# A graph attention layer: more of each tile's neighbour slots weighted by ScalarE, fewer by VectorE

## The reference

```
h = relu(layernorm(x))
g = (h @ W.T) as 8 heads of 32
score[i,j,head] = g[i].a_src + g[j].a_dst + adj[i,j]*We + be, only where adj[i,j] > 0
p = softmax over j of leaky_relu(score, 0.2)
out = x + sum_j p[i,j,head] * g[j,head,:] + h @ Wr.T + br
```

## Time and profile before

| | before |
|---|---|
| median of 3 runs | 2985.23 us (2981.51 to 2986.05) |
| profiled execution: its time | 2983.55 us |
| profiled execution: its span | 2982.0 us |
| mean granted TensorE clock | 0.682 of full speed |
| DVE busy over the span | 2407.1 us, 81% |
| POOL busy | 2003.5 us, 67% |
| ACT busy | 1625.0 us, 54% |
| PE busy | 1586.4 us, 53% |

### The profile page before, as it was taken

The page is one execution under the profiler, slowest core; times in us unless marked ns, Lnnn a source line. Parts: engine busy times, 40 slices in busy tenths (PEclk is TensorE's granted clock), DMA queues, the critical chain, the costliest instruction groups (busy, mean ns, idle before and its releaser), DMA issues.

```text
span 2982.0 us, 31982 instructions
## 1 busy us (share of the span) xinstructions
PE 1586.4 (53%) x5859; PEld 1067.1 (36%) x5860; DVE 2407.1 (81%) x5721; ACT 1625.0 (54%) x6849; POOL 2003.5 (67%) x1931
## 2 busy tenths in 40 slices
PE   7970043333436444565556666565656564526666
PEld 4650043323324332343333333333333332315445
DVE  3549576667868777899999999999999999189992
ACT  2220022223347555677778887786878775725444
POOL 3664777777777777777777777777777765254540
PEclk9995576666756666666666666666665666658888
DMA  3454533445454655566666767666666664264550
GB/s 98 147 184 139 174 110 109 115 121 161 130 158 140 182 161 170 163 196 198 194 197 196 217 205 214 203 206 209 208 208 212 206 205 145 106 166 106 130 141 2
DMA packets 254494, 486.91 MB, mean 163 GB/s; under 512 B 119232, under 2 KB 150464, under 8 KB 252144
## 3 DMA queue, kind: packets, MB, share of 16 engines
q1 hardware_dynamic: 151280, 319.60, 35.2%
q0 software_dynamic: 84752, 148.94, 18.8%
q10 hardware_dynamic: 18288, 16.65, 1.8%
HBM read 549.09 MB, written 25.76 MB: 193 GB/s over the span
## 4 chain that ended last, share of the span: by engine, by line
issue 29%; DMA 26%; POOL 20%; DVE 13%; PE 7%; ACT 2%; POOLq 1%; SPq 0%; DVEq 0%; ACTq 0%; PEldq 0%
DMA gath<-table,offs 24%; POOL gath L413 20%; DVE work L526 2%; PE banks L946 2%; DVE work L522 2%; DVE uleak L716 2%; DVE ushift L714 2%; PE banks L940 2%; ACT gath L808 2%; DMA adj_sb<-in_adj_dram 1%; PE banks L943 1%; DVE gath L698 1%; PE banks L1027 1%; PE banks L1017 1%; DVE adj_sb L698 1%
## 5 line engine op out<-in xcount | busy, mean ns | idle before, releaser
L413 POOL DMA_INDIRECT gath<-table,offs x1637 | 1718.6, 1050 | 604.8 <-issue 408.2
L808 ACT ACTIVATE gath<-gath,prob 128x32 f32<-128x32 f32 x6416 | 1366.4, 307 | 110.3 <-DVE prob L625 110.3
L969 PE MATMUL banks<-gath,ident 128*128 128x256 f32 x1670 | 513.3, 480 | 892.7 <-DVE gath L637 892.7
L976 PE MATMUL banks<-gath,ident 128*128 128x256 f32 x1604 | 630.0, 513 | 281.4 <-ACT gath L808 281.1
L969 PEld LDWEIGHTS banks<-gath,ident 128*128 128x128 f32 x1670 | 408.9, 249 | 1014.4 <-DVE gath L637 935.8
L526 DVE FIND_INDEX8 work<-work,adj_sb 128x8 uint32<-128x176 f32 (+30 forms) x833 | 645.5, 797 | 0.7 <-issue 0.6
L522 DVE MAX8 work<-adj_sb 128x8 f32<-128x176 f32 (+30 forms) x833 | 593.3, 788 | 11.0 <-DMA adj_sb<-in_adj_dram 11.0
L976 PEld LDWEIGHTS banks<-gath,ident 128*128 128x128 f32 x1604 | 327.9, 234 | 555.9 <-ACT gath L808 536.9
L803 ACT ACTIVATE prob<-pre 128x176 f32<-128x176 f32 (+23 forms) x63 | 23.7, 376 | 850.9 <-DVE pre L615 850.1
L437 POOL TENSOR_TENSOR gath<-gath 128x4096 f32<-128x4096 f32 x16 | 152.1, 9528 | 189.5 <-DMA gath<-dst_rows 189.5
L637 DVE TENSOR_TENSOR gath<-gath,prob 128x1024 f32<-128x1024 f32 (+8 forms) x171 | 240.2, 1456 | 2.1 <-issue 0.2
(11 more groups left out here) (111 smaller groups left out, 1788.5 us busy)
## 6 DMA issues: line engine op xcount, KB each, us to landing
adj_sb<-in_adj_dram SPq DMA_DIRECT2D x504, 512.0 KB
gath<-dst_rows SPq DMA_DIRECT2D x16, 2048.0 KB, 8.8
gath<-table,offs POOLq DMA_INDIRECT x1637
table<-gath POOLq DMA_DIRECT2D x32, 264.0 KB, 2.9
gath<-in_x_dram SPq DMA_DIRECT2D x32, 256.0 KB, 3.0
resid<-gath POOLq DMA_DIRECT2D x32, 256.0 KB, 2.6
work<-table SPq DMA_DIRECT2D x8, 1024.0 KB, 8.8
res_sb<-resid ACTq DMA_DIRECT2D x63, 128.0 KB
```

What stands on the lines that cost most here:

```text
L413: pool.indirect_dma_start(gath[:, ph.slot(b, k), :], None, table[:, :], bass.IndirectOffsetOnAxis(ap=offs[:, b, k:k + 1], axis=0), bounds_ ...
L808: last = s.activation(g, g, ACT.Copy, scale=prob[:, k * H + h:k * H + h + 1])
L969: last = m.matmul(ps_sum[:, b, :], ident[:, :], gath[:, ph.slot(b, k), 0:HD], start=False, stop=False)
L976: last = m.matmul(ps_sum[:, b, :], ident[:, :], gath[:, ph.slot(b, k), 0:HD], start=False, stop=(k == K - 1))
```

## The change

`act_slots` follows one formula instead of four cases, and the exponential gets one more wait.

```diff
-        self.act_slots = 10 if self.K < 20 or self.K > 38 else 14 if self.K < 32 else 16
+        self.act_slots = min(self.K // 2 + 6, 18)
```

```diff
                 c, K = j + ph.c0, ph.K
+                if ph.act_before:
+                    act.wait_ge(S["act_weighted"], ph.act_before)
                 act.wait_ge(S["z_ready"], c + 1)
                 s.activation(prob[:, 0:K * H], pre[:, b, 0:K * H], ACT.Exp).then_inc(S["exped"], 1)
```

## The result

The changed kernel took 3016.82 us (median of 4 runs, 3014.53 to 3020.07), against 2985.1 us of the kernel before in the same session: a ratio of 1.0116, with a 95% interval of 1.0104 to 1.0128. The kernel is 31.7 us slower; the prediction said 45.6 us slower, and its range of 3014 to 3046 holds the time.

The account below looks back on a forecast made before the run. The prediction took GpSimd to bound tiles 1 to 18 and, after the change, ScalarE from tile 19 on. Its terms -5.4 + 6.5 + 24 + 20.5 + 0 summed to +45.6 us, a median of 3031 us, range 3014 to 3046.

Parts of the forecast that it names:

- What bounds what: GpSimd's gathers set the pace in tiles 1 to 18, VectorE from tile 29 on; tiles 19 to 28 lie between.
- the handover: ScalarE's time between two tiles' weightings: copy, store, exponential and VectorE's normalization; 2.2 us for K of 20 to 23, 2.1 below.
- +24: Tiles 29 to 60: ScalarE becomes later than VectorE, making the stretch 24 us longer, bounds +20 and +30.
- ScalarE's cycle: Tiles 29 to 60: ScalarE's time per tile, slots of 1.704 us plus 2.2 us, 31.2 us with 17 slots.
- Tiles 19 to 28: 37 more slots on ScalarE exceed its idle time there: +6.5 us, bounds +1 and +9.
- The tail: Tiles 61 to 63: ScalarE is already late, so 12 added slots of 1.704 us count in full, +20.5 us.
- The wait: The new wait before ScalarE's exponential asks for weightings already ended: 0 us, bounds 0 and +2.5.
- Part 3: Tiles 1 to 18: gathers lose 22% beside VectorE's multiplying, so 24.5 us less of it gives -5.4 us, bounds 0 and -9.
- Rival (c): GpSimd gains more than 22% from the removed multiplications, towards the whole 24.5 us: 3013 to 3020 us; 7%.
- the forecast's own 3018: Lower end of the range, 3018 to 3043 us, for ScalarE as the bound from tile 19 on; 78%.
- Rival (a): ScalarE keeps up and VectorE's bound stretches gain: about 2965 us, needing at most 0.187 us per activation; 4%.

Follow-up runs that it names:

- mid_only: The kernel before with the formula and the new wait, slots changed only in tiles 19 to 60: 3008.79 us, ratio 1.0106.
- wait_only: The kernel before with the new wait on ScalarE's own weightings and nothing else: 2975.29 us, ratio 0.9997.
- five_early: The kernel before with VectorE's weighting in tiles 1 to 18 cut into parts of 5 to 7 slots, no slots moved: 2956.41 us, ratio 0.9925.

## Why the prediction was right, and where it was wrong

- **What bounds what**: right. GpSimd in tiles 1 to 18, VectorE from 29 on, and ScalarE's idle as the quantity that decides. The slack of 173.4 us over 32 tiles looked enough for much of the 184 us added; less the handover and without lending between tiles it gave +24, and the trace gave +23.0.
- **ScalarE's cycle**, 17 x 1.704 + 2.2 = 31.2 us: 31.1 measured. The handover had been read between three tiles at the very end, where ScalarE was already late, and held in 30 of the 32 tiles of this stretch (2.0 to 2.25 us); in tiles 19 to 28 it was 2.2 to 2.6.
- **Tiles 19 to 28**, +6.5: 4.9 in the changed kernel, 7.7 in mid_only. Traces in which these tiles are unchanged differ by 3 us (318.6 to 321.8), so neither is off.
- **The tail**, +20.5: 20.5, and 20.4 alone. Twelve of 249 slots made nearly two thirds of the net loss.
- **The wait**, 0: shown by wait_only. Its reason had one number wrong: between the end of the last weighting and the exponential, the tail before the change has 0.7 us (2569.94 to 2570.64), not over 1, which was still enough. Expecting VectorE to wait at L619 for some 3 us per tile was too much; it was 56.8 / 32 = 1.8 us in tiles 29 to 60.
- **Part 3 failed, the term of the gathers beside VectorE: -5.4 with a bound of -9, against -15.2 in the stretch.** The step that failed is "Eight gathers at 1.67 us apart instead of 1.30 lose 22% of the stretch": it made a share of the multiplying time out of what is a period set by the part. Taking a slot from a part of 6 lowers the gather's period from 1.67 to 1.40 us, so the loss falls from 0.37 to 0.10. The row that would have told it stood beside the others: the period of the gathers, 1.67 us, was the period of the parts, 13.43 / 8 = 1.68 us. A second weighting with other parts would have excluded a fixed share: in tile 1 of the kernel before, with parts of 8 slots (2285 ns), the gathers are 2.20 us apart and lose 41%, as GpSimd's rows in time show:

```profile
391.98 1.90 POOL L413 DMA_INDIRECT gath<-table,offs  x1 [0.30 <-issue]
394.19 1.90 POOL L413 DMA_INDIRECT gath<-table,offs  x1 [0.30 <-issue]
```

  Rival (c), with 7%, is where the time fell, and it had the direction: GpSimd gained more than the 22%. Its reason, the first gather, is a part of it only: the first gathers of the weightings lost 17.2 us before and 12.1 after, 5 of the 18 us that all gathers gained. The period set by the part, which gives the rest, stood in no branch of the prediction.

That the stated range holds the time is in part luck: 3016.82 is under the forecast's own 3018, and only the room left for (c) takes it in. Of the total error of 14 us, 11 are this term and its start a microsecond early; the rest is 1.6 in tiles 19 to 28 and 1 in 29 to 60.

Rival (a) would have needed activations of under 0.187 us; they start every 0.213 us in the changed kernel too (126 in 26.80 us).

## What to carry to other kernels

These are conclusions from this one kernel. Before moving work between two engines, find the one place in the trace where the receiving engine is already late, read its cycle there, and compare that cycle with the tile's, tile by tile: idle time summed over tiles cannot be lent between them, and at the end of the pipeline there is none. And when an instruction of one engine slows another's, compare periods before shares: if they are equal, try the size of the instruction. Here a size just above what the other needs was worth 0.75% (five_early) with no work moved at all.

## What the runs showed of the hardware

- While VectorE multiplies two SBUF operands in instructions back to back, GpSimd issues one indirect gather per such instruction of 1.40, 1.67, 2.21 or 3.27 us, and one per two of 0.87 or 1.13 us, although it needs 1.30 us alone. Shorter instructions on VectorE are therefore not always gentler to GpSimd: parts of 1.40 us gained 0.75%, parts of 1.13 us nothing. The Trainium skill, SBUF — State Buffer, section SBUF: two separate sides, describes an exclusive lock of the shared port pair that is held for the whole instruction, by a VectorE instruction with two SBUF inputs only against a GpSimd instruction that reads SBUF. That no second gather passes within one instruction agrees with it. The prediction read such a block as one over the whole multiplying time, and so as refuted by gathers that are merely slowed; a block of one instruction at a time lets one gather through at each boundary, as the rows show. That a gather ready too late for one boundary waits for the next is what the periods of 1.74 and 2.27 us add. No run here shows the port itself, nor whether the gather's issue reads SBUF.
- TensorE follows ScalarE's slots in pairs of matmuls with gaps, and with more of these the mean granted clock fell: from 0.65 to 0.60 in tiles 19 to 28, from 0.62 to 0.60 in 29 to 60 and from 0.69 to 0.57 in the tail, that is, with a larger share of the time at its lower level of 1.2 GHz than at 2.4 GHz. TensorE's busy time rose from 1586.4 to 1816.6 us for the same 5859 matmuls; in tiles 29 to 60, where it is busy for 664.41 of 936.54 us, it still waited for ScalarE's slots 415 times.
